# Time mixing of a perceiver layer: second state passes moved behind the mixes, gate product behind the low-rank product

## The reference

```
delta = x[previous token] - x
z     = tanh((x + delta * mu_x) @ Wx1)            # 5 x 32 columns
mus   = z[i] @ Wx2[i]   for i in 0..4             # five mixes r, w, k, v, g
r, k, v, g = (x + delta * m_i) @ W_i
decay = exp(-exp(tanh((x + delta * mw) @ Ww1) @ Ww2 + bw))
for each token t:                                 # per head: 32 heads, state 4 x 8
    kv = outer(k_t, v_t)
    o_t = r_t . (S + bonus * kv)
    S  = S * decay_t + kv
o = groupnorm(o) * gn_w + gn_b                    # over the 8 values of a head
out = (o * silu(g)) @ Wo
```

## Time and profile before

| | us |
|---|---|
| median of 3 runs | 2761.27 |
| the profiled execution's own time | 2759.83 |
| its span | 2758.0 |
| TensorE products busy in the span | 2485.8 (90%) |
| VectorE busy | 1981.7 (72%) |
| ScalarE busy | 1666.9 (60%) |
| GpSimd busy | 1203.0 (44%) |

### The profile page before, as it was taken

How to read it: one execution, slowest core, us unless ns; L and a number is a source line. 1 busy time by engine, 2 the same in 40 slices (tenths; PEclk the granted TensorE clock), 3 DMA queues, 4 the chain that set the end, 5 groups by cost and what they waited for, 6 DMA issues and landing times. The chain is left out here.

```text
span 2758.0 us, 51019 instructions
## 1 busy us (share of the span) xinstructions
PE 2485.8 (90%) x14035; PEld 2021.0 (73%) x14035; DVE 1981.7 (72%) x4330; ACT 1666.9 (60%) x3281; POOL 1203.0 (44%) x1935
## 2 busy tenths in 40 slices
PE   8999999999979967999999999999967777928998
PEld 6777777777758867998989889899833443526886
DVE  7999999999956636776767667677625666767886
ACT  6777777777745535666656666666634344315776
POOL 2211111011157624555555555555535655616775
PEclk9999999999989989999999999999977887868999
DMA  3000000000022215443434434344320010011111
GB/s 122 23 23 25 25 26 26 26 26 26 19 57 68 62 47 148 115 124 105 125 107 111 115 109 121 110 123 113 89 65 0 23 46 23 31 70 43 52 51 39
DMA packets 234985, 183.49 MB, mean 67 GB/s; under 512 B 37169, under 2 KB 226834, under 8 KB 234258
## 3 DMA queue, kind: packets, MB, share of 16 engines
q1 hardware_dynamic: 234770, 180.90, 22.9%
HBM read 152.74 MB, written 28.06 MB: 66 GB/s over the span
## 5 line engine op out<-in xcount | busy, mean ns | idle before, releaser
L255 DVE TENSOR_REDUCE kn_ssq<-kn_sq 128x8 f32<-128x1024 f32 x514 | 620.6, 1215 | 71.8 <-ACT kn_sq L197 67.3
L197 ACT ACTIVATE kn_sq<-kn_keys 128x1024 f32<-128x1024 f32 x514 | 527.9, 1027 | 177.4 <-PE kn_keys L146 174.9
L146 PE MATMUL kn_keys<-kn_wk_hi,kn_ct_hi 128*128 128x512 f32 x1028 | 334.2, 406 | 1.0 <-ACT kn_sq L197 1.0
L146 PE MATMUL kn_keys<-kn_wk_lo,kn_ct_hi 128*128 128x512 f32 x1028 | 320.2, 393 | 0.0
L146 PE MATMUL kn_keys<-kn_wk_hi,kn_ct_lo 128*128 128x512 f32 x1028 | 320.0, 392 | 0.0
L1012 DVE CUSTOM_DVE_ANT_0 ca_sc<-ca_b_sc,ca_rk,ca_rq_rows 128x257 f32<-128x257 f32 x512 | 230.8, 482 | 82.6 <-issue 82.0
L967 ACT ACTIVATE ca_sc<-ca_sc,ca_low 128x257 f32<-128x257 f32 x512 | 254.4, 499 | 12.7 <-DVE ca_low L1045 4.8
L1115 POOL TENSOR_TENSOR ca_sc<-ca_sc,ca_rden 128x1028 f32<-128x1028 f32 x128 | 243.3, 1901 | 10.0
L146 PEld LDWEIGHTS kn_keys<-kn_wk_lo,kn_ct_hi 128*128 128x128 f32 x1028 | 193.3, 188 | 44.5
L146 PEld LDWEIGHTS kn_keys<-kn_wk_hi,kn_ct_lo 128*128 128x128 f32 x1028 | 193.3, 188 | 43.7
L146 PEld LDWEIGHTS kn_keys<-kn_wk_hi,kn_ct_hi 128*128 128x128 f32 x1028 | 165.0, 189 | 69.9 <-ACT kn_sq L197 56.3
(11 more groups left out here) (316 smaller groups left out, 6754.7 us busy)
## 6 DMA issues: line engine op xcount, KB each, us to landing
ca_rk<-key_norms SPq DMA_DIRECT2D x512, 128.5 KB, 2.9
kn_rows<-in_ctx_dram SPq DMA_DIRECT2D x128, 128.0 KB, 2.3
ca_rows<-in_ctx_dram SPq DMA_DIRECT2D x128, 128.0 KB, 2.7
ca_xT<-normed_columns SPq DMA_DIRECT2D x16, 512.0 KB, 4.6
ca_vs_rows<-last_values SPq DMA_DIRECT2D x96, 64.0 KB, 2.6
qn_x<-in_x_dram SPq DMA_DIRECT2D x32, 128.0 KB, 2.5
normed_columns<-qn_xT_hi SPq DMA_DIRECT2D x32, 128.0 KB, 1.8
normed_columns<-qn_xT_lo SPq DMA_DIRECT2D x32, 128.0 KB, 1.8
```

The source lines that it names most:

```text
L146: mm = pe.matmul(keys[c][:, n * 512:(n + 1) * 512], a, w[:, c * CH + n * 512:c * CH + (n + 1) * 512], start=first, stop=last)
L197: act.activation(sq[c][:, :], keys[c][:, :], ACT.Square).then_inc(sq_ready, 1)
L255: dve.tensor_reduce(ssq[s][:, t * H + c * (H // 2):t * H + (c + 1) * (H // 2)], sq[c][:, :].rearrange("p (h d) -> p h d", d=P), AX.X, ALU. ...
```

## The change

The orders of all engines within a step are rewritten, and two kinds of buffer go from two to four.

- VectorE: only the first out and in pass of group j-1 stay among the mixes. Passes 1 to 3 follow the tenth mix. The variance comes first in the step.
- ScalarE: `statistics` is cut in two, `sums` and `squares`. Sums stand behind `std`, squares behind the tanh of the decay, `normalise` between the reads of the second and third token. `low_rank(j+1)` comes ahead of the exponential and of `gates`.
- TensorE: `columns(j+1)` comes right behind `project(j, 0)` and ahead of `output`; `low_rank(j+1)` comes ahead of `gates(j)`. `low_rank` now waits for all eight reads of the projections, `gates` for the two tanh reads of `low_rank`, and the next `decay` and `project` for the reads of the gates.
- GpSimd: `outer` and `own_values` of tokens 0 to 2 are made at the end of the group's own step, those of token 3 in the next step; `mean` and `inverse_std` stand among and behind the mixes.
- Sync queue: loads are issued one group earlier in the queue.

```diff
-        prod = [sb(f"prod{n}", [P, NH, HV, HQK + 1]) for n in range(2)]
-        kv = [sb(f"kv{n}", [P, NH, HV, HQK]) for n in range(2)]
+        prod = [sb(f"prod{n}", [P, NH, HV, HQK + 1]) for n in range(T)]
+        kv = [sb(f"kv{n}", [P, NH, HV, HQK]) for n in range(T)]
...
             load(2)
+            load(3)
             for j in range(GROUPS):
-                if j + 3 < GROUPS:
-                    load(j + 3)
+                if j + 4 < GROUPS:
+                    load(j + 4)
                 store(j)
...
             def low_rank(j):
                 pe.wait_ge(xp_ready, 2 * (j + 1))
-                ge(pe, sg_ready, 2 * j)
+                ge(pe, rk_taken, T * j)
+                ge(pe, v_taken, T * j)
...
             def decay(j):
                 pe.wait_ge(xm_ready, NM * j + 2)
+                ge(pe, sg_ready, 2 * j - 1)
...
                 for f in range(2):
-                    pe.wait_ge(rk_taken if f == 0 else v_taken, T * (j + 1))
+                    if live(j + 1):
+                        pe.wait_ge(z_ready, 2 * (j + 1) + f + 1)
+                    else:
+                        pe.wait_ge(rk_taken if f == 0 else v_taken, T * (j + 1))
...
                     project(j, 0)
+                if live(j) and live(j + 1):
+                    columns(j + 1)
                 if live(j - 2):
                     output(j - 2)
                 if live(j):
-                    if live(j + 1):
-                        columns(j + 1)
                     for t in range(1, T):
                         project(j, t)
+                    if live(j + 1):
+                        low_rank(j + 1)
                     gates(j)
-                if live(j + 1):
-                    low_rank(j + 1)
...
+                if live(j + 2):
+                    sums(j + 2)
                 if live(j):
                     decay(j)
+                if live(j + 2):
+                    squares(j + 2)
...
-                    for t in range(1, T):
+                    take(j, n, 1)
+                    if live(j + 2):
+                        normalise(j + 2)
+                    for t in range(2, T):
                         take(j, n, t)
+                    if live(j + 1):
+                        low_rank(j + 1)
                     act.wait_ge(rk_taken, T * (j + 1))
...
                     gates(j, n)
-                if live(j + 1):
-                    low_rank(j + 1)
-                if live(j + 2):
-                    statistics(j + 2)
-                    normalise(j + 2)
```

More of the change, by code:

```diff
@@ L1287, in project @@
                 ge(pe, v_taken, T * j + t)
+                if t == 0:
+                    ge(pe, sg_ready, 2 * j)
                 for a in range(2):
@@ L1347, in _, with sums @@
         def _(act):
-            def statistics(j):
+            def sums(j):
                 n = j % 2
@@ L1354, in statistics, with squares @@
                 s.then_inc(sum_ready, 1)
+            def squares(j):
+                n = j % 2
                 act.wait_ge(nmean_ready, j + 1)
@@ L1440, in _ @@
             for j in range(2):
-                statistics(j)
+                sums(j)
+                squares(j)
                 normalise(j)
@@ L1486, in scan_in @@
                     ge(dve, o_turned, 2 * (j - 1))
-                dve.tensor_reduce(o[n][:, t, :].rearrange("p (h v) -> p h v", v=HV), prod[t % 2][:, :, :, :], AX.X, ALU.add).then_inc(scan, 1)
+                dve.tensor_reduce(o[n][:, t, :].rearrange("p (h v) -> p h v", v=HV), prod[t][:, :, :, :], AX.X, ALU.add).then_inc(scan, 1)
                 dve.wait_ge(scan, c + 2)
                 dve.wait_ge(kv_ready, T * j + t + 1)
-                dve.tensor_tensor(state, state, kv[t % 2][:, :, :, :], ALU.add).then_inc(scan, 1)
+                dve.tensor_tensor(state, state, kv[t][:, :, :, :], ALU.add).then_inc(scan, 1)
             def own_weight(j, t):
@@ L1527, in mixes, with out, into @@
                             mixing(j, k)
-                if before:
-                    scan_out(j - 1, 1 - n, 0)
+                def out(t):
+                    if before:
+                        scan_out(j - 1, 1 - n, t)
+                def into(t):
+                    if before:
+                        scan_in(j - 1, 1 - n, t)
                 if back:
@@ L1532, in step @@
                 mixes(0, 1)
-                if before:
-                    scan_in(j - 1, 1 - n, 0)
+                out(0)
+                mixes(2, 3)
                 if back:
                     inverse_root(j - 2)
[L1537 to L1546, removed]
+                into(0)
+                mixes(4, 5, 6, 7, 8, 9)
                 if back:
                     gate(j - 2, n)
-                if before:
-                    scan_in(j - 1, 1 - n, 2)
+                out(1)
+                into(1)
                 if now and live(j + 1):
                     shift(j + 1)
-                if before:
-                    scan_out(j - 1, 1 - n, 3)
+                out(2)
                 if now:
                     own_weight(j, 0)
+                into(2)
                 if back:
                     residual(j - 2, n)
-                if before:
-                    scan_in(j - 1, 1 - n, 3)
+                out(3)
                 if now:
-                    for t in range(1, T):
-                        own_weight(j, t)
+                    own_weight(j, 1)
+                    own_weight(j, 2)
+                into(3)
+                if now:
+                    own_weight(j, 3)
             dve.memset(mhalf[:, :], -0.5).then_inc(const_ready, 1)
@@ L1583, in _, with mean @@
             pool.wait_ge(const_ready, 5)
-            def statistics(j):
+            def mean(j):
                 pool.wait_ge(sum_ready, j + 1)
@@ L1635, in mixes @@
                             mixing(j, n, k)
-                if before:
-                    own_values(j - 1, 1 - n, 0)
-                    own_values(j - 1, 1 - n, 1)
                 mixes(0, 1, 2, 3)
@@ L1641, in step @@
                     normed(j - 2, n)
-                mixes(4)
-                if before:
-                    outer(j - 1, 1 - n, 2)
-                    own_values(j - 1, 1 - n, 2)
-                mixes(5, 6, 7)
+                mixes(4, 5)
+                if live(j + 2):
+                    mean(j + 2)
+                mixes(6, 7, 8, 9)
+                if live(j + 2):
+                    inverse_std(j + 2)
+                if now:
+                    own_products(j, n, 0)
                 if before:
@@ L1649, in step @@
                     own_values(j - 1, 1 - n, 3)
-                mixes(8, 9)
                 if now:
-                    own_products(j, n, 0)
                     own_products(j, n, 1)
```

18 lines of the change are left out of this document (9 added, 9 removed).

## The result

The changed kernel takes 2716.66 us (median of 4 runs, 2714.79 to 2719.26) against 2761.51 for the one before in the same comparison (4 runs, 2760.64 to 2761.88). The ratio is 0.9839, with a 95% interval of 0.9822 to 0.9856. The forecast was 2721, range 2698 to 2742.

The account below looks back on a forecast made before the run. It took the stage to be bound by waits inside a loop, not by an engine. Terms of -0.1, -14.0, -28.9 (four turns of -7.2), -0.8 and +3.8 sum to -40 us, giving 2721 us, range 2698 to 2742.

Parts of the forecast that it names:

- The stall and its removal: VectorE's variance waits 11.7 us for ScalarE's square, queued behind statistics and normalisation; the change moves those earlier.
- LR to M: Start of TensorE's low-rank product to a group's first mix on VectorE: 10.15 us, against 14.33 plus 4.56 of gate product ahead.
- C to LR: Start of the next group's transposes to start of its low-rank product on TensorE: 12.25 us, about 1.3 of it inserted normalisation.
- M to C: First mix on VectorE to the next group's transposes on TensorE: taken as 21.5 us, between 16.1 and 23.1.
- removing VectorE passes gives nothing: From first mix to next transposes: at 1.2 GHz TensorE's products set the length, 23.1 us, whatever VectorE's passes.
- The variance's wait: VectorE's wait ahead of the variance in a steady turn: about 2.5 us, not 11.7.
- rival of half the gain: Work moved into ScalarE's middle becomes the new wait: turns of 48, about -19 us, 2742 us; chance 0.18.
- M(1) to M(2): First mix of group 1 to first mix of group 2 on VectorE: 38.8 us against 52.75, -14.0.
- M(6) to M(7): First mix of group 6 to that of group 7 on VectorE, without normalisation: 42.6 us against 43.41, -0.8.
- The tail: End of the stage, variance of group 6 to that of group 7: 25.3 us instead of 21.6, +3.8 with rounding.
- Full clock: Rival: no long idle remains in the loop, TensorE keeps 2.4 GHz, turns of 38.5, -78, 2683 us; chance 0.15.
- Slower by the clock: Rival: 1.2 GHz lasts through projects, output, transposes, low-rank and gate products; turns of 60.3, 2825 us; chance 0.04.

Follow-up runs that it names:

- one-part kernel: Kernel before, with only sums, squares, normalisation and GpSimd's mean and inverse deviation moved earlier, and loads one group earlier: 2728.45 us, ratio 0.9896.
- the kernel whose clock mostly stays up: Changed kernel with eight of the ten mixing products on all 128 rows, weights zero outside their 32 rows: 2688.37 us, ratio 0.9744.
- the rest alone: Changed kernel with statistics and normalisation put back at the end of the step: 2762.97 us, ratio 1.0011.

## Why the prediction was right

*The stall and its removal.* Right in place and size. LR to M is 10.28 against 10.15 worked out from rows; the late thing behind it is the Silu of the gates, as written. The one-part kernel shows where most of the gain comes from: ScalarE's square out from behind the statistics. The gate product's move, which the prediction counted within this stretch, is worth nothing by itself.

*C to LR.* 12.15 against 12.25. Putting normalisation among the reads costs 1.07 (12.15 - 11.08), not 1.3.

*M to C.* The value taken, 21.5, was a choice between 16.1 at 2.4 GHz and 23.1 at 1.2 GHz. The seven stretches are 18.06 to 23.28, and both ends were right as ends: 23.0 to 23.3 where the clock is 0.55, and 16.1 to 17.8 in the kernel whose clock mostly stays up (0.89 to 0.92). Nothing in the rows of before gave the mean, so that 21.5 fell 0.4 from the measured 21.1 is luck: the clock is low for nearly all of some stretches and for part of the others. The forecast's own range, 2708 to 2731, is called the clock ends of this stretch, but only its upper end is one. With the sum's own lower ends (15.3 in turn 1 to 2, 16.1 in the five others) the time comes to about 2690. The sentence "removing VectorE passes gives nothing" holds at 1.2 GHz only. From M(0) to the end of the stage it is worth 5.2 us, and 7.4 with the clock up.

*The variance's wait.* Predicted 2.5, measured 3.5 to 6.3 in the turns before M(2) to M(7). In the turn of 45.45 VectorE arrives at 2162.23 - 4.34 = M + 39.97, as laid out (M + 40.2); in the faster ones the last mix is earlier, so VectorE has more slack than the 2.6 given. The rival of half the gain had ScalarE's middle as the new wait: squares started at 2130.98 = M + 13.1 (laid out M + 13), the affine at 2132.96 = M + 15.0 (M + 16.6), so that queue ran on time.

*Ends.* M(1) to M(2): 39.29 for 38.8. M(0) to M(1) lost 1.2 where 0.1 less was expected, since LR came 1.6 earlier and not 2.7, and M(6) to M(7) gained 3.2 for 0.8, since its M to C was a short one, 18.81. The tail: +5.0 for +3.8, of which the passes are +4.0 (25.59 - 21.56) as worked out; another +1.2, behind the second variance, was not foreseen. The last output product takes 6.45 us, 5.20 before. TensorE's wait shortly ahead of it is longer (13.9 us, 8.2 before), but that alone doesn't explain it: with the gates ahead of the low rank the wait is 15.0 and the same product takes 5.32. What sets the clock there stays open. The measured stage of 403.6, against 404 predicted, is closer than these steps deserve; their errors cancel.

*The clock.* "Full clock" held 0.15 and did not come: the granted clock of the stretches was 0.55 to 0.73 with TensorE idle for 1.2 to 1.4 us of each. The Trainium skill, TensorE: Matmul & The Clock Gate (HAM oscillation), has the clock fall in long gaps between bursts; the trace disagrees with it as the only rule. The Trainium skill has a second case on the same page (A second HAM failure mode: psum-queue depth-cycling), short idles between groups of products. That fits the falls better, but not the cure, since the products on 128 rows leave TensorE more idle (1.93 of 16.11 us at 0.89, 3.50 of 17.40 at 0.92). "Slower by the clock" did not come either: project 0 still runs at 1.2 GHz in the slow turns (1.22 for its first row, as in the earlier trace rows), and from the output product on (3.62) all is at 2.4 GHz.

*Parts.* They don't add: one alone -0.0104, the rest alone +0.0011, both -0.0161. The rest is worth something only once the square is not behind the statistics. Of this rest, the gate product gave nothing and the passes about 0.0028 when taken back alone. The transposes ahead of the output product, GpSimd's new order and the four buffers were never taken back alone, so their share is not shown.

## What to carry to other kernels

When an engine waits in a loop, follow the instruction that releases it back along its own queue: the statistics that stood ahead of the square were 7.8 of the 14.3 us from low-rank product to first mix, and the gates that stood ahead of it next were another 1.8. Moving work out of a stretch pays only as far as the next engine allows, so test two edits together as well as alone. And count the last turns by themselves: an order that serves the steady step cost 4 us in the tail, and the old order there won them back.

## What the runs showed of the hardware

In these kernels TensorE's granted clock rose when the mixing products used more rows. Groups of the mixing products, first of the changed kernel, then of the one with 128 rows; a line has its count, busy us, mean ns of one, and the idle time ahead:

```profile
L1271 PE MATMUL tm_b_t<-tm_z,tm_wx 32*128 32x512 f32 x128 | 82.7, 785 | 10.7 <-DVE tm_mix L1482 10.0 <-ACT tm_zl L1396 0.7
```

```profile
L1274 PE MATMUL tm_b_t<-tm_z,tm_wx 128*128 128x512 f32 x128 | 63.6, 622 | 12.8 <-DVE tm_mix L1485 12.1 <-ACT tm_zl L1399 0.7
```

As many products with as many columns and four times the rows, three quarters of them zeros, take 622 ns in place of 785. The products that the edit left alone speed up beside them, so it is the clock and not the product itself. The first layer of the decay, again first in the changed kernel:

```profile
L1277 PE MATMUL tm_b_a<-tm_xm,tm_ww 128*64 128x512 f32 x32 | 28.3, 1038 | 2.8 <-POOL tm_xm L1621 2.8
```

```profile
L1280 PE MATMUL tm_b_a<-tm_xm,tm_ww 128*64 128x512 f32 x32 | 17.1, 660 | 3.8 <-POOL tm_xm L1626 3.8
```

At the lower level TensorE had been busy without a gap, 19.00 of 19.00 us at 0.50, so an idle engine was not what held the clock down there. With two of ten products still on 32 rows the stretch is at 0.89 to 0.92, and with the square, the normalisation and the tail changed as well, the turn from M(5) to M(6) is at 1.00 throughout. What quantity the chip goes by was not measured: the products and their weight loads went to 128 rows together. The runs show only that this edit raised the clock while TensorE's idle time in the stretch grew, and that in this layer it was worth 28 us by the medians, 26 by the ratios (0.9839 to 0.9744).
